# The mixture stages over gathered rows of chosen pairs instead of over all tokens

## The reference

```python
x = x + 0.5 * L0_ffn(layernorm(x))      # stage a: 8 experts, each takes its 1024 best tokens
x = x + L0_attn(layernorm(x))           # stage b
x = x + 0.5 * L0_ffn(layernorm(x))      # stage c
x = x + 0.5 * L1_ffn(layernorm(x))      # stage d
x = x + L1_attn(layernorm(x))           # stage e
x = x + 0.5 * L1_ffn(layernorm(x))      # stage f
```

```python
scores = softmax(x @ gate_w.T)                     # (4096, 16)
# the best 2 of 4 groups of experts, in them the best 4 experts of each token
c[token, expert] = scores if chosen else 0         # 4 of 16 are not 0
h1, h3 = x @ w1[e], x @ w3[e]                      # for every expert e
y = sum over e of c[:, e] * ((silu(h1) * h3) @ w2[e])
z = (silu(x @ ws1) * (x @ ws3)) @ ws2
return y + z
```

## Time and profile before

| | us |
|---|---|
| median of 3 runs (4503.84 to 4511.96) | 4505.9 |
| the profiled execution, its own time | 4506.45 |
| its span, first to last instruction | 4504.7 |
| stage d, first DMA issued to last add issued and stored | 1914.6 to about 2603 |
| stage f, the same | 3815.8 to 4504.7 |

### The profile page before, as it was taken

The page is one execution under the profiler, slowest core; times in us unless marked ns, Lnnn a source line. Parts: engine busy times, 40 slices in busy tenths (PEclk is TensorE's granted clock), DMA queues, the critical chain, the costliest instruction groups (busy, mean ns, idle before and its releaser), DMA issues. The chain is left out here.

```text
span 4504.7 us, 73929 instructions
## 1 busy us (share of the span) xinstructions
PE 4003.0 (89%) x26222; PEld 3087.4 (69%) x26222; DVE 2518.9 (56%) x4852; ACT 2003.3 (44%) x3837; POOL 956.5 (21%) x716
## 2 busy tenths in 40 slices
PE   4599959988974699879999969999999997899999
PEld 4499835555544599768888846666656664788888
DVE  4644346655645544356555546665666555565555
ACT  1566524444440666522333346555565554233332
POOL 0244312211200244313333300000000000133332
PEclk9999969999995799979999979999999999899999
DMA  3343210000003333210000010000000001000001
GB/s 116 94 102 78 35 53 15 15 21 16 25 26 102 117 82 80 33 52 15 10 11 14 24 61 1 11 10 11 1 11 10 11 6 41 20 11 10 14 10 38
DMA packets 144880, 159.27 MB, mean 35 GB/s; under 512 B 20320, under 2 KB 132704, under 8 KB 144352
## 3 DMA queue, kind: packets, MB, share of 16 engines
q1 hardware_dynamic: 117728, 113.15, 7.8%
q0 software_dynamic: 26880, 42.48, 5.0%
HBM read 105.01 MB, written 50.59 MB: 35 GB/s over the span
## 5 line engine op out<-in xcount | busy, mean ns | idle before, releaser
L1971 ACT ACTIVATE e_prob<-e_s_ps,e_small 128x512 f32<-128x512 f32 x512 | 346.7, 684 | 169.5 <-DVE e_small L2082 84.8
L2082 DVE TENSOR_REDUCE e_small<-e_s_ps 128x2 f32<-128x1024 f32 x256 | 313.2, 1223 | 168.3 <-PE e_s_ps L1848 164.3
L1388 ACT ACTIVATE b_pt<-b_t_ps 128x1024 f32<-128x1024 f32 (+3 forms) x256 | 180.8, 706 | 312.0 <-PE b_t_ps L1320 310.9
L903 POOL TENSOR_TENSOR f_h_lo<-f_hid,f_h_hi 128x512 fp32r<-128x512 f32 x144 | 188.2, 1307 | 518.2 <-ACT f_h_hi L874 518.2
L903 POOL TENSOR_TENSOR d_h_lo<-d_hid,d_h_hi 128x512 fp32r<-128x512 f32 x144 | 188.2, 1307 | 499.6 <-ACT d_h_hi L874 499.6
L2060 POOL TENSOR_TENSOR e_wide<-e_small,const 128x512 f32<-128x512 f32 x64 | 66.5, 1039 | 999.3 <-DVE e_small L2155 999.3
L1882 PE MATMUL e_z_ps<-e_pt,e_v 128*64 128x512 f32 x1024 | 275.5, 617 | 0.4 <-DVE e_zf L2162 0.4
L1861 PE MATMUL e_t_ps<-const,e_prob 128*128 128x128 f32 x2048 | 267.8, 274 | 6.1 <-ACT e_pt L1960 5.3
L1861 PEld LDWEIGHTS e_t_ps<-const,e_prob 128*128 128x128 f32 x2048 | 234.5, 141 | 51.1 <-issue 17.1
L1571 DVE TENSOR_REDUCE b_small<-b_s_ps 128x2 f32<-128x1024 f32 (+3 forms) x256 | 209.6, 819 | 84.7 <-PE b_s_ps L1299 80.7
L60 PE MATMUL d_h_ps<-d_x_hi,d_w_hi 128*128 128x512 f32 x576 | 231.0, 401 | 0.0
(11 more groups left out here) (544 smaller groups left out, 11832.4 us busy)
## 6 DMA issues: line engine op xcount, KB each, us to landing
ae_raw<-w_dram SPq DMA_DIRECT2D x16, 1024.0 KB
ce_raw<-w_dram SPq DMA_DIRECT2D x16, 1024.0 KB
d_raw<-m_dram SPq DMA_DIRECT2D x54, 128.0 KB, 2.3
...
```

The lines of the kernel that those rows point to most:

```text
L903: gp.tensor_tensor(h_lo[:, g % 2], hid[:, g % 2], h_hi[:, g % 2].bitcast(F32), ALU.subtract).then_inc(hid_lo, 1)
L1388: act.activation(pt[:, kt % 2, a, :, 0:width], t_ps[:, :, 0:width], ACT.Exp).then_inc(p_ready, 1)
L1971: act.activation(prob[:, at], s_ps[:, at], ACT.Exp, bias=nmx[:, at:at + 1], accum_out=sums[:, buf, h * QT + s:h * QT + s + 1]).then_inc(p_ ...
L2082: dve.tensor_reduce(nmx[:, at:at + 2], s_ps[:, at:at + 2], AX.X, ALU.max, negate=True).then_inc(mx_ready, 1)
```

## The change

`moe` gets a new body; nothing else but two DRAM buffers in `program` is touched.

- **Front.** All 8 groups are normalised in place (two of four tiles on DVE, two on POOL), stored to `xn_rows`, turned and given logits, with no expert work in between. Then `choose` runs in one piece on DVE, followed by new work: `places` ranks each chosen pair of token and expert within its expert (two PE matmuls with a triangle and with ones, scans over the counts) and gives it a slot in a list in which each expert's pairs fill whole tiles of 128; `lists` makes the inverse, the token of every slot, with 128 one-hot products on PE whose operands DVE makes (32 groups of one 128x512 and four 128x144 instructions), and `owner_i`, the expert of every tile. The weights of all 16 experts are brought in and split once (`w_hi` on ACT, `w_lo` on POOL) and stay on chip.
- **Tile loop** (`over_tiles`, 144 tiles whatever the data, 8 to a loop body). POOL gathers the 128 rows of tile j from `xn_rows` into one of 8 buffers `xg`. PE turns them (2 transposes), 6 matmuls of 128x256 give both hidden halves (tokens stationary, weights moving), the hidden tile is turned (1 transpose), 3 matmuls of 128x256 give the output. The address of the weights is read by PE's sequencer from `owner_i` (`value_load`), once for up and once for down in each step. A step holds turn of tile j, up of j-1, turn of hidden j-2 and down of j-3. ACT and DVE make high and low parts, silu and product, and copy the output to `y` in turns; SP stores four tiles at a time to `o_rows`.
- **Gather back.** When all of `o_rows` is stored, POOL gathers for each of 32 token tiles the four rows of its pairs (128 gathers) into `takes`, four token tiles deep. Beside it PE, ACT and DVE compute the shared part for 8 groups, and DVE adds shared part and four rows each to the input (`collect`), which SP stores.

```diff
-def moe(nc, tag, x_in, x_out, gate_w, w1, w3, w2, const):
+HCOL = 2 * INTER
+UCOL = KC * HCOL + D
+
+COLS, BODY = 144, 8
+
+
+def moe(nc, tag, x_in, x_out, xn_rows, o_rows, gate_w, w1, w3, w2, const):
...
-        xs = sb("xs", [P, NT, D])
-        x_hi, x_lo = sb("x_hi", [P, KC, TOK], F32R), sb("x_lo", [P, KC, TOK], F32R)
+
+        big = sb("big", [P, 16 * NT * E1])
+        w_hi, w_lo = sb("w_hi", [P, E1 * UCOL], F32R), sb("w_lo", [P, E1 * UCOL], F32R)
+        raw = sb("raw", [P, 2, UCOL])
+        xh, xl = sb("xh", [P, 2 * KC * GTOK], F32R), sb("xl", [P, 2 * KC * GTOK], F32R)
+        xg = sb("xg", [P, BODY, D])
...
-        def over_units(eng, unit):
-
-            with eng.Fori(1, UNITS // 2 - 1) as i:
-                unit(0, i * (2 * NG), i * 2, True)
-                unit(1, i * (2 * NG) + NG, i * 2 + 1, True)
-            unit(0, (UNITS - 2) * NG, UNITS - 2, True)
-            unit(1, (UNITS - 1) * NG, UNITS - 1, False)
+        def over_tiles(eng, step):
+
+            for u in range(BODY):
+                step(u, u)
+            with eng.Fori(1, COLS // BODY) as i:
+                for u in range(BODY):
+                    step(i * BODY + u, u)
+            for u in range(3):
+                step(COLS + u, u)
...
+            sp.wait_ge(token_ready, 1)
+            for g in range(2):
+                sp.dma_start(xr[:, g], xv[:, g * GT:(g + 1) * GT]).then_inc(xs_in[g], 16)
+            for n in range(COLS // GT):
+                sp.wait_ge(y_act, n * GT + GT)
+                sp.wait_ge(y_dve, n * GT + GT)
+                half_ = n % 2
+                sp.dma_start(rv[:, n * GT:(n + 1) * GT], y[:, half_ * GT:(half_ + 1) * GT]).then_inc(stored[half_], 16)
...
+        @block.gpsimd
+        def _(gp):
+            gp.wait_ge(norm_ready, 1)
+            for g in range(NG):
+                for t in range(g * GT + 2, g * GT + GT):
+                    last = gp.tensor_scalar(xs[:, t], xs[:, t], mean[:, t:t + 1], rstd[:, t:t + 1], ALU.subtract, ALU.mult)
+                last.then_inc(xn_pool, 1)
+            for u in range(E1):
+                gp.wait_ge(w_hi_done, u + 1)
+                gp.tensor_tensor(expert_w(w_lo, u), raw[:, u % 2], expert_w(w_hi, u).bitcast(F32), ALU.subtract).then_inc(w_lo_done, 1)
+            gp.wait_ge(xn_stored, 16 * NG)
+            gp.wait_ge(token_ready, 1)
+            for j in range(COLS):
+                if j >= BODY:
+                    gp.wait_ge(t_ready, j - BODY + 1)
+                gp.indirect_dma_start(out=xg[:, j % BODY], out_offset=None, in_=xn_rows,
+                                      in_offset=bass.IndirectOffsetOnAxis(ap=token_i[:, j:j + 1], axis=0)).then_inc(gathered[j % BODY], 16)
+            for half_ in range(2):
+                gp.wait_ge(stored[half_], 16 * (COLS // BODY))
+            for t in range(NT):
+                if t >= GT:
+                    gp.wait_ge(used, t - GT + 1)
+                for k in range(TOPK):
+                    gp.indirect_dma_start(out=takes[:, t % GT, k], out_offset=None, in_=o_rows,
+                                          in_offset=bass.IndirectOffsetOnAxis(ap=back[:, k, t:t + 1], axis=0)).then_inc(taken[t % GT], 16)
...
+            def step(j, u):
+                if within(j, 1):
+                    up_at = pe.value_load(owner_i[0:1, at(j - 1)], min_val=0, max_val=(E1 - 1) * UCOL)
+                if within(j, 3):
+                    down_at = pe.value_load(owner_i[0:1, at(j - 3)], min_val=0, max_val=(E1 - 1) * UCOL)
+                if within(j, 0):
+                    pe.wait_ge(gathered[u], uses(j, u) + 16)
+                    if past(j, 2):
+                        pe.wait_ge(x_lo_done, j - 1)
                     for k in range(KC):
+                        last = pe.transpose(pa[:, u % 2, k * P:(k + 1) * P], xg[:, u, k * P:(k + 1) * P], ident)
+                    last.then_inc(t_ready, 1)
+                if within(j, 1):
+                    m, s = j - 1, (u - 1) % BODY
+                    pe.wait_ge(x_lo_done, m + 1)
+                    if past(m, 2):
+                        pe.wait_ge(hid_ready, m - 1)
+                    for k in range(KC):
+                        last = mm3(pe, ph[:, s % 2, 0:HCOL], x_tile(xh)[:, s % 4, k], x_tile(xl)[:, s % 4, k],
+                                   w_hi[:, ds(up_at + k * HCOL, HCOL)], w_lo[:, ds(up_at + k * HCOL, HCOL)], k == 0, k == KC - 1)
+                    last.then_inc(h_ready, 1)
+                if within(j, 2):
+                    m, s = j - 2, (u - 2) % BODY
+                    pe.wait_ge(hid_ready, m + 1)
+                    if past(m, 2):
+                        pe.wait_ge(h_lo_done, m - 1)
+                    pe.transpose(pt[:, s % 2, 0:P], hid_tile[:, s % 2], ident).then_inc(ht_ready, 1)
+                if within(j, 3):
+                    m, s = j - 3, (u - 3) % BODY
+                    pe.wait_ge(h_lo_done, m + 1)
+                    if past(m, 2):
+                        pe.wait_ge(*copied(m - 2, s))
+                    mm3(pe, po[:, s % 2, 0:D], h_tile(hh)[:, s % 4], h_tile(hl)[:, s % 4],
+                        w_hi[:, ds(down_at + KC * HCOL, D)], w_lo[:, ds(down_at + KC * HCOL, D)], True, True).then_inc(o_ready, 1)
...
+            pe.wait_ge(chosen_ready, 1)
+            pe.matmul(pt[:, 0], lower[:], chosen[:], start=True, stop=True)
+            pe.matmul(pt[:, 1], ones[:], chosen[:], start=True, stop=True).then_inc(ranked, 1)
+            for n in range(HOT_GROUPS):
+                pe.wait_ge(hot_ready, n + 1)
+                for m in range(4):
+                    last = pe.matmul(po[:, 0, 0:COLS], hot_row[:, n % 3, m], hot_col[:, n % 3, m], start=(n == 0 and m == 0),
+                                     stop=(n == HOT_GROUPS - 1 and m == 3), skip_group_check=True)
+                last.then_inc(hot_used, 1)
+            pe.wait_ge(token_ready, 1)
+            pe.wait_ge(owner_ready, 1)
+            pe.wait_ge(w_lo_done, E1)
+            over_tiles(pe, step)
...
+            for g in range(NG + 1):
+                if g < NG:
+                    pe.wait_ge(xn_in[g % 2], 16 * (g // 2 + 1))
...
+            def step(j, u):
+                if within(j, 0):
+                    act.wait_ge(t_ready, j + 1)
+                    if past(j, 4):
+                        act.wait_ge(h_ready, j - 3)
+                    copy(x_tile(xh)[:, u % 4], pa[:, u % 2, 0:D].rearrange("p (k c) -> p k c", k=KC), x_hi_done)
+                if within(j, 1):
...
-        @block.gpsimd
-        def _(gp):
-            def unit(b, first, u, more):
-                for g in range(NG):
-                    gp.wait_ge(hid_hi, first + (g + 1))
-                    gp.tensor_tensor(h_lo[:, g % 2], hid[:, g % 2], h_hi[:, g % 2].bitcast(F32), ALU.subtract).then_inc(hid_lo, 1)
...
+
+                for n in range(HOT_GROUPS):
+                    k, t0 = n * 4 // NT, n * 4 % NT
+                    if n >= 3:
+                        dve.wait_ge(hot_used, n - 2)
+                    dve.tensor_tensor(hot_row[:, n % 3], iota[:, 0:P].unsqueeze(1).to_broadcast([P, 4, P]),
+                                      row[:, k, t0:t0 + 4].unsqueeze(2).to_broadcast([P, 4, P]), ALU.is_equal)
+                    for m in range(4):
+                        t = t0 + m
+                        last = dve.tensor_scalar(hot_col[:, n % 3, m], iota[:], col[:, k, t:t + 1], ids[:, t:t + 1],
+                                                 ALU.is_equal, ALU.mult)
+                dve.tensor_copy(token_i[:], po[:, 0, 0:COLS]).then_inc(token_ready, 1)
...
+                if within(j, 0):
+                    dve.wait_ge(x_hi_done, j + 1)
+                    dve.tensor_tensor(x_tile(xl)[:, u % 4], pa[:, u % 2, 0:D].rearrange("p (k c) -> p k c", k=KC),
+                                      x_tile(xh)[:, u % 4].bitcast(F32), ALU.subtract).then_inc(x_lo_done, 1)
...
+            def collect(g):
+
+                dve.wait_ge(zo_ready, g + 1)
+                dve.wait_ge(xs_in[g % 2], 16 * (g // 2 + 1))
+                for t in range(GT):
+                    part = po[:].rearrange("p b (t d) -> p (b t) d", d=D)[:, t]
+                    last = dve.scalar_tensor_tensor(xr[:, g % 2, t], part, 0.5, xr[:, g % 2, t], ALU.mult, ALU.add)
+                last.then_inc(zo_used, 1)
+                dve.wait_ge(zo_used, g + 1)
+                for t in range(GT):
+                    n = g * GT + t
+                    dve.wait_ge(taken[t], 16 * TOPK * (g + 1))
+                    for k in range(TOPK):
+                        last = dve.scalar_tensor_tensor(xr[:, g % 2, t], takes[:, t, k], coef[:, k, n:n + 1], xr[:, g % 2, t],
+                                                        ALU.mult, ALU.add)
+                        if k < TOPK - 1:
+                            st.link(last)
+                    last.then_inc(used, 1)
+
             dve.wait_ge(gw_ready, 1)
...
+            choose()
+            places()
+            lists()
+            over_tiles(dve, step)
```

593 lines of the change are left out of this document (342 added, 251 removed).

## The result

The changed kernel took 4874.8 us (median of four runs, 4870.7 to 4878.0) against 4504.9 for the kernel before (4503.7 to 4512.0): 1.082 times as long, 95% interval 1.080 to 1.084. The forecast was 4322 us, the range 4215 to 4620. The change is slower, and by more than the range allowed. The profiled execution has a span of 4876.2 us, 371.5 more than before. Columns of the stretches: length, busy time (instructions) by engine, granted clock (1.00, the highest in the rows, is called the upper clock here, 0.50, the lowest, the lower), DMA share, GB/s.

A forecast was written before the change was run, and what follows sets the result against it. Stages d and f were taken as bound by PE. Per stage, 164 us to the first tile, 235 tile loop and 198 gather back make 597 against 689, 92 less, twice 184: 4322 us, range 4215 to 4620.

The forecast's parts named there:

- the sequencer's rate, 2L + 0.8 with L = 0.3: Tile loop: PE's sequencer, with two address loads a step at price L each, needs 1.4 us a tile.
- the slowest sets the period: Tile loop: four rates compete; slowest 1.45 us, a tenth added, 1.6 us a tile, 235 us with fill and drain.
- the 0.8: Tile loop: the constant in us added to two loads in the rate of PE's sequencer per step.
- The first rival: Tile loop: a dear address load makes the kernel slower; at L = 1.0 period 2.8, loop 408, total 4668 us; 18%.
- point of decision, a period of 2.24: Tile loop: period in us, at L = 0.72, from which the dear address load decides that the kernel is slower.
- The 0.15 in the chances: Tile loop: case of a load between 0.3 and 1.0 us, total 4438 us, counted under faster by more; chance 0.15.
- The chain from DVE's collect of one group to the next about 12 us ... covered: Gather back: the shared part's chain per group hides beside 23 us of gathers and costs nothing more.
- the forecast of 198: Gather back: wait for the last store, 128 gathers at 1.45 us (186 us), then landing, adds and store: 198 us.
- Routing: Choice, slots, lists and owners on DVE before the tile loop: 92 us (88 to 118), covering the weight split.
- the price of 0.69: Routing: time in us taken for most DVE instructions of 512 columns in the choice.
- Front: Stage's start to the choice: 24 us, then 48 us for eight logits groups, two of them at the lower clock.
- The rival in which PE stays at the lower clock: Tile loop: routing leaves PE idle 90 us, so a tile costs 2.7 us, the stage about 765, total 4658; 7%.

The follow-up runs named there:

- early down products: Changed kernel, but in the shared part PE makes the down products of group g-1 before turning group g and making its up products, not after: 4757.6 us.

## Why the prediction was wrong

- **The step that failed: the sequencer's rate, 2L + 0.8 with L = 0.3, 1.4 us beside PE's 1.45, and "the slowest sets the period".** Measured, the steady tile is 1.40 + 2 x 0.65 = 2.69 us, so both terms were mis-sized: a load is 0.65 and the rest 1.40, whether this rest is PE's own time, to which the loads add (then "the slowest sets the period" is wrong), or the sequencer's (then the 0.8 is); the runs don't settle that. L = 0.3 stood for the load alone, and the fetch is indeed 0.30 to 0.33, far from the 2.9 us of a store's landing, but its two test instructions (0.23) were not counted. No run shows the 0.8 for the rest of a step, which was the author's estimate; what the runs show in its place is the 1.40. Over the loop: 242.6 / 144 = 1.68 us a tile with no load, plus 0.56 for each. Together 404 against 235 us, in two stages 339 of the 553 us by which the whole was missed (4874.8 - 4322).
- **The first rival** had the right place: its period of 2.8 and loop of 408 us are what came, though by luck of two errors, a load of 0.65 and not of 1.0, and a rest of 1.4 and not of 0.8. Its point of decision, a period of 2.24, was passed. Its total of 4668 us was still 207 short, because it kept the other parts of the forecast. It had 18%. Its counter-argument, that round trips on the chip take under 0.3 us, is nearly true of the fetch (0.30) and beside the point.
- **The 0.15 in the chances** stood for a load between the forecast's 0.3 us and the first rival's 1.0, with a total of 4438 us; no row of before shows its size. The runs show 0.54 to 0.65 for a load with its tests, and less for the fetch alone (0.30 by its record, 3.40 for ten). So that case had the load about right and failed on the 0.8: with 1.40 for the rest the tile is 2.69 us, not 2.0.
- **"The chain from DVE's collect of one group to the next about 12 us ... covered".** It was 30 us. The gathers were cheaper than taken (1.25, not 1.45), which by the working gives 172 us for the last part. It took 262, and with early down products still 204, so some 30 us were missing from the working beside the ring: there the first gather starts 11 us behind the last tile's transposes, not 3, and after the first 16 gathers POOL waits 17 us for the first collect. Against those 204 us the forecast of 198 is near by two errors that cancel. Of the 58 us that early down products took off, 24 are the order and 31 the late counts. I had added the chain's operations, but not followed the buffer `hh` back to the products that read it, nor seen that these stand behind the next group's up products. That miss is some 64 us a stage.
- **Routing.** 108.5 us against 92, in the range of 88 to 118. The slow operations beside POOL are shown (16 us); the price of 0.69 came from rows without such a neighbour. The lists took 1.66 us a group (32 of them from 2045.5 to 2098.6) instead of 1.43.
- **Front.** 89 us against 72: all eight groups of logits ran at the lower clock (0.50, a group every 7.67 us), not two. The working had the 7.7 us of such a group and chose wrongly how many.
- **The clock in the loop.** The rival in which PE stays at the lower clock did not come: the granted clock was 0.98 in spite of 63% PE work.
- **Stage e.** 27 us that no step held. The prediction took all other stages as unchanged.
